# Attention of a two-layer gated block: value products issued for four heads at a time instead of two

## The reference

```python
qkv = (x @ w_qkv.T).reshape(B, N, 3, H, D).transpose(2, 0, 3, 1, 4)   # x normalised; N = 256, H = 16, D = 16
k = jnp.concatenate([extra_k, k], axis=2)                             # 77 + 256 = 333 keys
v = jnp.concatenate([extra_v, v], axis=2)
attn = jax.nn.softmax(jnp.einsum('bhnd,bhmd->bhnm', q * scale, k), axis=-1)
out = jnp.einsum('bhnm,bhmd->bhnd', attn, v)                          # the value products
out = out.transpose(0, 2, 1, 3).reshape(B, N, C) @ w_proj.T + b_proj
```

## Time and profile before

| | us |
|---|---|
| median of three runs | 1472.48 |
| span of the profiled execution | 1466.6 |
| second attention, first scores to last value block | 749 to 1149 |
| batch 0 of it | 69.8 |
| batches 1 to 6 | 280.3 (46.7 each) |
| batch 7 | about 47 |

### The profile page before, as it was taken

How to read it: one execution, slowest core, us unless ns; L and a number is a source line. 1 busy time by engine, 2 the same in 40 slices (tenths; PEclk the granted TensorE clock), 3 DMA queues, 4 the chain that set the end, 5 groups by cost and what they waited for, 6 DMA issues and landing times. The chain is left out here.

```text
span 1466.6 us, 30458 instructions
## 1 busy us (share of the span) xinstructions
PE 1334.5 (91%) x8152; PEld 1054.1 (72%) x8152; DVE 823.1 (56%) x2153; ACT 709.9 (48%) x1871; POOL 528.0 (36%) x589
## 2 busy tenths in 40 slices
PE   5999899999999999999167899999998899999998
PEld 4886667777777777777054677676765789999997
DVE  7979814333333333333346577676768576666666
ACT  2444644444444444444043787777866444444443
POOL 1003353333333333331666666776451110111110
PEclk9999999999999999999568999999999999999999
DMA  4023116677576657642432121222110000000000
GB/s 108 0 88 94 40 46 189 210 218 222 160 216 178 176 161 222 191 120 91 133 111 84 47 63 59 58 58 62 51 67 16 23 15 15 9 7 14 15 8 15
DMA packets 105407, 134.03 MB, mean 91 GB/s; under 512 B 29587, under 2 KB 89331, under 8 KB 105299
## 3 DMA queue, kind: packets, MB, share of 16 engines
q1 hardware_dynamic: 62339, 59.05, 13.7%
q0 software_dynamic: 15456, 48.62, 12.0%
q10 hardware_dynamic: 27504, 25.05, 5.0%
HBM read 100.66 MB, written 32.01 MB: 90 GB/s over the span
## 5 line engine op out<-in xcount | busy, mean ns | idle before, releaser
L741 POOL DMA_INDIRECT xg<-n_rows,idx x191 | 181.2, 949 | 296.5 <-DVE wS L2105 220.4
L1242 PE MATMUL ps<-wgu,xT 128*128 x764 | 259.1, 462 | 0.3 <-ACT xT L1061 0.3
L1242 PE MATMUL ps<-wdn,hT 88*128 (+1 forms) x892 | 227.9, 380 | 2.4 <-ACT hT L1019 1.8
L2264 DVE TENSOR_REDUCE nmx<-ps 128x1 f32<-128x333 f32 x256 | 127.3, 498 | 118.6 <-PE ps L1242 96.7
L1120 ACT ACTIVATE pD<-ps,nmx 128x333 f32<-128x333 f32 x256 | 139.2, 546 | 98.1 <-DVE nmx L2264 74.1
L1242 PEld LDWEIGHTS ps<-wdn,hT 88*128 88x128 f32 x892 | 154.3, 190 | 20.6 <-issue 5.2
L2108 DVE TENSOR_TENSOR hC<-sg,ps 128x176 f32<-128x176 f32 x191 | 64.5, 338 | 172.9 <-ACT sg L1071 144.7
L1242 PEld LDWEIGHTS ps<-wgu,xT 128*128 128x128 f32 x764 | 130.0, 190 | 41.7 <-issue 0.8
L771 POOL DMA_INDIRECT yg<-y_rows,slotG x128 | 123.5, 965 | 88.2 <-issue 36.2
L2111 DVE COPY hT<-ps 88x256 f32<-88x256 f32 x191 | 80.3, 421 | 132.6 <-issue 82.9
L1552 PE MATMUL ps<-ident,pD 128*128 128x128 f32 x768 | 130.8, 281 | 23.9 <-DVE pT L2270 15.2
(11 more groups left out here) (306 smaller groups left out, 2996.5 us busy)
## 6 DMA issues: line engine op xcount, KB each, us to landing
y_rows<-yC ACTq DMA_DIRECT2D x191, 128.0 KB
wgu<-in_wgu SPq DMA_DIRECT2D x64, 352.0 KB
wdn<-in_wdn SPq DMA_DIRECT2D x64, 176.0 KB
xg<-n_rows,idx POOLq DMA_INDIRECT x191
kraw<-in_kD SPq DMA_DIRECT2D x8, 308.0 KB
x<-in_x SPq DMA_DIRECT2D x4, 512.0 KB, 4.5
n_rows<-nB SPq DMA_DIRECT2D x4, 512.0 KB, 4.3
yg<-y_rows,slotG POOLq DMA_INDIRECT x128
```

The source lines that it names most:

```text
L741: pool.indirect_dma_start(out=xg[:, b % XS, :], out_offset=None, in_=n1_rows, in_offset=bass.IndirectOffsetOnAxis(ap=idx[:, b:b + 1], axis ...
L1242: return pe.matmul(o, lhsT, rhs, start=start, stop=stop, **kw)
L2264: dve.tensor_reduce(nmx[:, k:k + 1], ps[:, score_bank(k), 0:NK1], AX, ALU.max, negate=True).then_inc(d_mx, 1)
```

## The change

Four heads are issued in a block (`HPV` = 4), again chunk by chunk, one in each column quarter: 12 matmuls, 24 records. A block then stands at steps 9, 17, 25 and at step 1 of the next batch: 4 a batch, 32 in all. The order of heads becomes 0, 2, 4, 6, 1, 3, 5, 7 and the same again from 8. `pT` gets 5 slots, given out by a table, and three small tensors and nT move into regions of SBUF that are used in turns, which makes the room. The order of units 8 and 9 is swapped (the query rows of pairs 4 and 5 are now read until step 27's scores, which are issued at step 24), and the waits for finished rows stand at scores 0, 4, 16 and 20 instead of 0, 8, 16 and 24.

```diff
@@ -28,9 +28,11 @@
 HP1 = H1 // 2
 NPAR = P // (2 * DH1)
 HG1 = 8
-HPV = 2
+HPV = 4
 HQ = P // 32
-ORDER = [4 * g + h for g in range(H1 // 4) for h in (0, 2, 1, 3)]
+ORDER = [8 * g + 2 * q + e for g in range(H1 // 8) for e in range(2) for q in range(HQ)]
+PT_SLOTS = 5
+PT_SLOT = (0, 1, 2, 3, 4, 0, 2, 3, 1, 0, 3, 4, 2, 1, 3, 4)
 NG1 = H1 // HG1
 UNITS = 4 + HP1
 NK1 = NKEY + SEQ
...
@@ -124,13 +126,9 @@
-        nT = sb("nT", [P, 2, DC, P])
-        idx = sb("idx", [P, NBLK], I32)
-        slot_row = sb("slot_row", [1, NBLK], I32)
-        exp_row = sb("exp_row", [1, NBLK], I32)
...
@@ -208,7 +206,7 @@
-            pT = s("pT", [P, 2 * HPV, 3, SEQ])
+            pT = s("pT", [P, PT_SLOTS, 3, SEQ])
...
@@ -258,6 +256,7 @@
+            nT = s("nT", [P, 2, DC, P])
...
@@ -271,6 +270,9 @@
+            idx = s("idx", [P, NBLK], I32)
+            slot_row = s("slot_row", [1, NBLK], I32)
+            exp_row = s("exp_row", [1, NBLK], I32)
...
@@ -431,7 +433,13 @@
             return -1 if j < U_K else U_K - 1 if j < U_ROWS else U_Q if rows_of(j)[0] else U_K
         VALUES_AFTER = 2
+        ROWS_NEEDED_AT = (0, 4, 16, 20)
         SCORE_BANKS = (0, 1, 7)
+
+        def pT_before(n):
+
+            same = [m for m in range(n) if PT_SLOT[m] == PT_SLOT[n]]
+            return same[-1] if same else max(m for m in range(H1) if PT_SLOT[m] == PT_SLOT[n]) - H1
         def score_bank(k):
             return SCORE_BANKS[k % AHEAD]
...
@@ -443,7 +451,7 @@
         def rows_of(j):
             is_q = 1 - (j - U_ROWS) % 2
-            return 1 - is_q if j >= UNITS - 2 else is_q, 2 * ((j - U_ROWS) // 2)
+            return 1 - is_q if j >= UNITS - 4 else is_q, 2 * ((j - U_ROWS) // 2)
         REC_AT, COPY_AT, DEN_AT, ATT_AT = 0, 3, 5, 6
         REDUCE_AT, SUMS_AT, VE_AT, RSTD_AT = (9, 11, 14, 16), (13, 15), 20, 28
...
@@ -1123,8 +1131,8 @@
             def d_copy_pT(b, k):
                 h, t = k // TB, k % TB
                 act.wait_ge(d_pt, STEPS * b + k + 1)
-                after(act, d_pv, H1 * b + h - 2 * HPV + 1)
-                act.copy(pT[:, h % (2 * HPV), :, t * P:(t + 1) * P], ps[:, 5 + k % 2, 0:3 * P].rearrange("p (c n) -> p c n", c=3)).then_inc(d_eva, 1)
+                after(act, d_pv, H1 * b + pT_before(h) + 1)
+                act.copy(pT[:, PT_SLOT[h], :, t * P:(t + 1) * P], ps[:, 5 + k % 2, 0:3 * P].rearrange("p (c n) -> p c n", c=3)).then_inc(d_eva, 1)
             def d_copy_group(b, g):
                 act.wait_ge(d_pv, H1 * b + HG1 * (g + 1))
...
@@ -1535,8 +1543,8 @@
             def d_scores(b, k, s):
                 h, t = head_of(k), k % TB
-                if k % (TB * 4) == 0:
-                    pe.wait_ge(d_ea, UNITS * b + U_ROWS + 2 * (k // (TB * 4)) + 2)
+                if k in ROWS_NEEDED_AT:
+                    pe.wait_ge(d_ea, UNITS * b + U_ROWS + 2 * ROWS_NEEDED_AT.index(k) + 2)
                 if k == 0:
                     pe.wait_ge(d_ck, CK * (b + 1))
...
@@ -1565,7 +1573,7 @@
                     for n in range(h0, h0 + HPV):
                         h = ORDER[n]
                         at = 32 * (h // 2 % HQ)
-                        last = mm(ps[at:at + 32, 4, 0:SEQ], v1[0:rows, s, c, h // 2, 2 * (h % 2):2 * (h % 2) + 2, :].rearrange("p a d -> p (a d)"), pT[0:rows, n % (2 * HPV), c, :],
+                        last = mm(ps[at:at + 32, 4, 0:SEQ], v1[0:rows, s, c, h // 2, 2 * (h % 2):2 * (h % 2) + 2, :].rearrange("p a d -> p (a d)"), pT[0:rows, PT_SLOT[n], c, :],
                                   c == 0 and h % 2 == 0, c == 2 and h % 2 == 1, skip_group_check=True)
                         if c == 2:
                             last.then_inc(d_pv, 1)
...
@@ -2266,8 +2274,8 @@
             def d_copy_pT(b, k):
                 h, t = k // TB, k % TB
                 dve.wait_ge(d_pt, STEPS * b + k + 1)
-                after(dve, d_pv, H1 * b + h - 2 * HPV + 1)
-                dve.tensor_copy(pT[:, h % (2 * HPV), :, t * P:(t + 1) * P], ps[:, 5 + k % 2, 0:3 * P].rearrange("p (c n) -> p c n", c=3)).then_inc(d_evd, 1)
+                after(dve, d_pv, H1 * b + pT_before(h) + 1)
+                dve.tensor_copy(pT[:, PT_SLOT[h], :, t * P:(t + 1) * P], ps[:, 5 + k % 2, 0:3 * P].rearrange("p (c n) -> p c n", c=3)).then_inc(d_evd, 1)
             def d_rec_group(b, g):
                 dve.wait_ge(d_exp, STEPS * b + TB * HG1 * (g + 1))
```

## The result

The changed kernel takes 1458.94 us (median of 6 runs, 1457.65 to 1464.85) against 1469.62 (6 runs, 1466.41 to 1472.70): ratio 0.9935, 95% interval 0.9922 to 0.9949. It is 10.7 us faster where 30.0 were forecast. The time lies inside the range of 1428 to 1461 and the sign is right; the size is not. (The level moved a little too: I started from a median of 1472.5 us, which is 1469.6 with the three later runs.

A forecast was written before the change was run, and what follows sets the result against it. PE was taken as the bound, 93% busy in batches 1 to 6. Batches 1 to 5 gain 5 x 4.7 - 2.0 = 21.5 us, with batches 6, 7 and 0 30.0: 1472.5 - 30.0 = 1442.5 us, range 1428 to 1461.

The forecast's parts named there:

- Term 1: Value blocks on PE: 64 become 32 at the same 1.57 us each, removing 50.2 us of PE time.
- Rival 2: Value blocks: the array serves only two streams at once, 9 us of PE time saved, 1467 us; chance 0.09.
- How much of it reaches the end: Second attention: of 6.28 us of blocks removed per batch, 4.7 us, 75%, shortens the batch.
- Steps 0 to 7: First piece of a batch: PE falls to 9.8 us, others at most 8.03 (POOL 9.43), so 1.4 us gained.
- Steps 16 to 23: Third piece of a batch: ACT's 10.13 us of busy time limits it, so 0.8 of 1.57 us gained.
- Steps 24 to 31: Last piece of a batch: steps PE reaches early wait for their exponentials, so 1.1 us gained.
- Term 2: POOL's chain to the second sum, DVE at step 15: 1.0 us lost in batches 2 and 4, 2.0 in all.
- Moved at no cost: Earlier waits for rows, fifth slot, units 8 and 9 swapped: value zero, swap bounded at 0.56 us a batch.
- Batches 0, 6 and 7: Second attention's other batches: gains of 1.8 us in batch 0, 4.2 in batch 6, 2.5 in batch 7.
- Rival 3: PE's granted clock falls as PE waits more: up to 30 us slower, 1502 us; chance 0.06.
- rival 1: ACT, DVE and POOL take over at once; only steps 0 to 15 gain, 14 us in all, 1458; chance 0.15.
- Signs that were named: Profile after: block about 1.5 us, batches 1 to 6 at 253 to 256 us, their clock 0.97 or more.

The follow-up runs named there:

- e8: Changed kernel with twelve of sixteen gathers of batches 1 to 4 in their second half and without three of POOL's four additions: 1427.37 us, one run.
- e7: Kernel before without three of POOL's four additions a row: 1448.89 us, ratio 0.9989.
- e5: Kernel before with only the order of two row units swapped: 1449.94 us, ratio to the kernel before 0.9992.
- e15: Changed kernel with twelve of sixteen gathers late and half of ACT's query casts left out in batches 1 to 7: 1460.37 us, ratio to before 0.9923.
- e12: Changed kernel with twelve of sixteen gathers of batches 1 to 4 in the second half, on the chip without stalls: 1427.13 us, one run.
- e10: Kernel before, unchanged, profiled on the chip without stalls: 1452.09 us, one run.
- e9: Changed kernel itself, nothing edited, on the chip without stalls: 1433.76 us, ratio to the kernel before 0.9873.
- e16: Changed kernel itself, nothing edited, on a chip with stalls: 1458.98 us, ratio to the kernel before 0.9921.
- e4: Changed kernel without three of POOL's four additions a row, gathers as they were, on a chip with stalls: 1448.49 us, ratio to before 0.983.
- e14: Changed kernel with twelve of sixteen gathers late and value products in blocks of two heads, chip with stalls: 1479.05 us, ratio to before 1.0062.
- e13: Changed kernel with twelve of sixteen gathers of batches 1 to 4 in the second half, chip with stalls: 1470.75 us, ratio to before 0.9988.
- e1: Changed kernel with blocks of two heads again, its order, slots and earlier waits kept: 1467.95 us, ratio to the kernel before 0.9962.

## Why the prediction was wrong, step by step

**Term 1, right.** 50.2 us forecast, 100.6 to 52.1 measured, a block 1.50 us. Four quarters ran beside each other at no more than two had cost. Rival 2 is out. The estimate from the Trainium skill's figure for three column tiles ("TensorE: Matmul & The Clock Gate", Part 3), 10 us dearer, is out as well.

**How much of it reaches the end: this is the step that failed.** I took 4.7 us a batch for batches 1 to 5, 75% of what PE loses. e8 against e7 it is 16.5 us for the five, and 2.8 of them are the swap of the units (e5, taken to be worth the same here; no run separates it in the changed kernel). The blocks give 13.7, 2.7 a batch, 44%. By pieces of eight steps, as means of the five batches, they give 0.7, 1.4, 0.1 and 0.4 (1.0 with the swap), where I took 1.4, 1.4, 0.8, 1.1:
- Steps 0 to 7: "others at most 8.03, almost all comes through". I read busy shares there. DVE's share was low, but one of its instructions was held by POOL in step 3 of the even batches, and steps 0 and 6 grew too.
- Steps 16 to 23: the reason was right and the size was not. The casts of ACT (seen in e15, where half of one takes 0.6 us off step 16) and the wait in step 22 give back 1.45 of the block's 1.6. Batch 2 of e12 against e10 seems to confirm my 0.8, with 1.0; but 0.85 of that is step 16 of the kernel before, which POOL's additions had lengthened (e7).
- Steps 24 to 31: 0.4. Steps 30 and 31 grew by 0.6 to 0.7, and step 24 is only 0.25 shorter, where the swap alone made it 0.57.

**Term 2: wrong place, and nearly the right size by luck.** I expected DVE to wait for POOL's second sum. It did not: the sum ended at 892.34 and DVE came at 893.57. The additions cost time on their way, by holding DVE's small instruction in step 14. That cost 1.3 us in batches 1, 2 and 4 and 0.4 in batch 3, with 0.14 in each step 16: 5.0 us, and e9 less e12 gives 5.1 over the four batches. But in the kernel before they cost 1.9 already (e10 less e7), in another step, so what the change adds is 2.5 over batches 1 to 5 (4.4, e9 less e8, less 1.9), where I had charged 2.0. The even and odd pattern that I had built on the earlier trace rows was of no use.

**Stalls: not in the sum at all.** On chips that have them the changed kernel takes 179.9 (first profile) and 180.6 us (e16) for batches 1 to 4, on B 172.5: 7.4 to 8.1 us, nearly all at step 20. The kernel before had 185.1 in its profile and 182.9 on B, 2.2. So about 5 of the forecast 30 us went there. In the traces POOL is late after its additions and sends its gathers in a row beside the block of step 17; in e4, on a chip with stalls but without the additions, step 20 is 2.16.

**Moved at no cost: right in the sum, by luck.** The swap gives 0.57 us in each batch, just the bound of 0.56, and 2.1 in batch 6. Batch 0 gives 2.9 back, and the whole of e5 is 1.3 us, not told from zero.

**Batches 0, 6 and 7.** Batch 6: 4.2 forecast, 4.6 measured, but 2.1 of it is the swap, and the blocks alone gave 2.1 there (e14 against e13). Batch 7: 2.5 forecast, 0.3 measured up to the last scores; DVE is busy 35.9 of 44.0 us there and the clock fell from 0.96 to 0.88. On B it is the same pair of clocks and 44.3 us both times; where the clock was 0.92 (e12) the stretch took 43.6. Batch 0: 1.8 forecast, 4.9 longer in the two profiles and 0.9 longer on B, where the granted clock over it went from 0.88 to 0.80 with less work on PE. The 4.9 is mostly scatter of stalls: kernels with blocks of two had 75.1 (e1) and 72.7 us (e14) there. Rival 3 was thus half right in batch 7, and in batch 0, for which I hadn't priced it, and wrong in batches 1 to 6 (0.99).

**The rivals.** The measured 1458.9 is rival 1's 1458, and its account is nearer to the runs than mine: cover gone, and steps 0 to 15 gaining while 16 to 31 do not. e8 against e7 the blocks give 2.1 us a batch in steps 0 to 15 and 0.5 in 16 to 31. In batch 2 of the changed kernel itself both halves gained next to nothing, because the additions took the second piece and the stall the third. That its sum comes out to the microsecond is luck, as it knew of neither the stalls nor the swap. What took the forecast down in batches 1 to 5, from 21.5 to 9.1 us: blocks at 13.7 instead of 23.5, less 9.8; the swap, 2.8 more; the additions, 0.5 less; the stalls, 4.9 less.

**Signs that were named.** Block about 1.5 us: yes. Batches 1 to 6 253 to 256 us: 266.6, and 253.9 in e12, where the swap and the additions' old cost make up for the blocks. Steps 0 to 15 of batch 2 about 20: 22.5, and 21.1 in e8. Steps 16 to 31 about 20.5: 22.3, and 20.6 in e8. PE's idle time ahead of ACT's exponentials and casts: no, the largest part was for DVE's copies. DVE's second sum right at the end of POOL's: no, 1.2 us behind in batch 2. Clock: yes in batches 1 to 6. The batches shrank by 2.3 us each, and under 3 with a short block was the named sign that the forecast is wrong.

## What to carry to other kernels

Before pricing a block that goes, look at what the other engines do while it runs: an instruction that takes nine times its usual time beside another engine's work is free only as long as the block covers it. Busy shares don't show that; the durations of single instructions do. When a second cause is in play (here POOL's additions), take it out of both kernels: a comparison that takes it out of the new one alone counts its old cost as a gain of the change. If the removed time was a queue's slack, find which engine's work then runs together, and try its order again (here POOL's gathers), on more than one chip.

## What the runs showed of the hardware that I had not expected

- Four column quarters of fp32 matmuls with 32 columns each cost no more than two: 1.50 against 1.49 us a block, 24 records instead of 12.
- DVE instructions of 0.17 us took 1.47 to 1.54 beside POOL's addition on 128x512, and a pair of 128x256 went from 1.11 to 2.19 us beside POOL's products.
- On two of the experiments' three chips ACT and DVE started up to 3.4 us after PE's work had ended, both at the same moment, with several gathers going out on POOL; on the third the same programs showed no such wait. The kernel before was 21 us slower on the two (1472 against 1451); between its first profile and e10 (spans 1466.6 and 1450.3), 12.0 us lie in batch 0 (69.9 against 57.9). What holds the two engines was not found, and no run here tells whether it is the gathers' traffic or their issue.
